# Cross-attention and ternary FFN on one core: work taken batch by batch, six product tiles transposed by DMA as int16

## What is computed (the reference, cut)

```
q = ctx @ Wq.T + bq; k = ctx @ Wk.T + bk
x = x + layernorm(x) @ softmax(q @ k.T).T            # both per batch
bit_linear(x, w, b):
    gx = max|x| per row; xq = round(x * 127 / gx) * gx / 127
    gw = mean|w|;        wq = clip(round(w / gw), -1, 1) * gw
    return xq @ wq.T + b
h = layernorm(x)
p = silu(bit_linear(h, gate_w, gate_b)) * bit_linear(h, val_w, val_b)
out = x + bit_linear(p, out_w, out_b)
```

## Time and profile before

| quantity | value |
|---|---|
| median of 3 runs | 69.74 us (69.73 to 70.26) |
| profiled execution: its time, its span | 69.72 us, 67.6 us |
| instructions | 1258 |
| busy: PE, DVE, ACT, POOL | 83%, 71%, 70%, 75% of the span |
| read from HBM, written to HBM | 6.04 MB, 1.05 MB |

### The profile page before, as it was taken

The page is one execution under the profiler, slowest core; times in us unless marked ns, Lnnn a source line. Parts: engine busy times, 40 slices in busy tenths (PEclk is TensorE's granted clock), DMA queues, the critical chain, the costliest instruction groups (busy, mean ns, idle before and its releaser), DMA issues.

```text
span 67.6 us, 1258 instructions
## 1 busy us (share of the span) xinstructions
PE 56.4 (83%) x353; PEld 36.2 (54%) x356; DVE 47.7 (71%) x140; ACT 47.4 (70%) x84; POOL 51.0 (75%) x108
## 2 busy tenths in 40 slices
PE   3999959798977896359799999999999999999500
PEld 2775649486847683232335433453844547988300
DVE  2002338896599957199898899999999988965500
ACT  5311479999996998398878867579689596995000
POOL 5904990688849877897997869868999999999100
PEclk9999999999999999999999999999999999999999
DMA  0899999999951000000000000000000000006354
GB/s 0 194 336 248 361 255 315 393 422 422 410 196 43 10 5 0 5 0 0 0 5 0 0 0 0 0 0 0 0 10 0 0 0 0 0 0 200 112 172 146
DMA packets 3254, 7.20 MB, mean 107 GB/s; under 512 B 392, under 2 KB 1836, under 8 KB 3248
## 3 DMA queue, kind: packets, MB, share of 16 engines
q1 hardware_dynamic: 3248, 7.13, 30.5%
HBM read 6.04 MB, written 1.05 MB: 105 GB/s over the span
## 4 chain that ended last, share of the span: by engine, by line
PE 48%; DMA 16%; POOL 12%; SPq 8%; DVE 5%; issue 4%; DVEq 0%; POOLq 0%
DMA x<-in_x_tok 16%; PE psG L750 11%; PE psV L750 10%; PE psO L827 7%; PE psT L798 5%; SPq L196 4%; PE psH L827 4%; PE psV L745 3%; PE psG L745 3%; POOL prob L279 3%; POOL rstd L289 2%; DVE st L385 2%; PE psV L785 2%; POOL rstd L269 2%; PE psH L734 1%
## 5 line engine op out<-in xcount | busy, mean ns | idle before, releaser
L608 ACT ACTIVATE sil<-psG,s_gv 128x1024 f32<-128x1024 f32 x8 | 8.9, 1113 | 1.8 <-PE psG L750 1.6
L494 DVE TENSOR_REDUCE pmax<-prod 128x1 f32<-128x1024 f32 x8 | 9.5, 1208 | 0.0
L481 DVE TENSOR_TENSOR prod<-psV,sil 128x1024 f32<-128x1024 f32 x7 | 8.6, 1222 | 0.8 <-PE psV L750 0.7
L617 ACT ACTIVATE pT<-psT,unshift 128x1024 bf16<-128x1024 f16 x7 | 7.8, 1113 | 1.8 <-PE psT L798 1.3
L750 PE MATMUL psG<-ter_gate,hT 128*128 128x512 bf16 x29 | 7.6, 381 | 0.5 <-issue 0.3
L329 POOL TENSOR_SCALAR prod<-prod,pqs 128x1024 f32<-128x1024 f32 x7 | 7.8, 1115 | 0.0
L750 PE MATMUL psV<-ter_val,hT 128*128 128x512 bf16 x28 | 7.3, 382 | 0.0
L279 POOL TENSOR_SCALAR prob<-prob,resum 128x256 f32<-128x256 f32 x8 | 3.7, 475 | 3.4 <-DVE resum L397 3.4
L324 POOL TENSOR_TENSOR res<-x,bo_sb 128x256 f32<-128x256 f32 x8 | 5.7, 740 | 0.0
L680 PE MATMUL psT<-kT,qT 128*128 128x256 f32 x16 | 4.2, 392 | 1.3 <-ACT qT L557 1.3
L827 PE MATMUL psO<-ter_out,pT 128*128 128x256 bf16 x40 | 5.2, 273 | 0.0
(11 more groups left out here) (121 smaller groups left out, 148.0 us busy)
## 6 DMA issues: line engine op xcount, KB each, us to landing
w_gate<-in_w_gate SPq DMA_DIRECT2D x2, 512.0 KB, 5.9
x<-in_x_tok SPq DMA_DIRECT2D x2, 512.0 KB, 10.0
xt_sb<-in_x_T SPq DMA_DIRECT2D x2, 512.0 KB, 10.7
w_val<-in_w_val SPq DMA_DIRECT2D x2, 512.0 KB, 11.0
w_out<-in_w_out SPq DMA_DIRECT2D x2, 512.0 KB, 12.7
out_x<-res SPq DMA_DIRECT2D x8, 128.0 KB, 1.8
ctx_sb<-in_ctx_T SPq DMA_DIRECT2D x1, 384.0 KB, 3.9
bias_rows<-bh_part SPq DMA_DIRECT2D x9, 4.0 KB
```

The costliest lines, as they stand in the source:

```text
L481: nc.vector.tensor_tensor(prod[:, t % P_RING, :], psV[:], sil[:, t % S_RING, :], ALU.mult).then_inc(prod_done, 1)
L494: nc.vector.tensor_reduce(pmax[:, t:t + 1], prod[:, t % P_RING, :], AX.X, ALU.max, apply_absolute_value=True).then_inc(pmax_done, 1)
L608: nc.scalar.activation(sil[:, t % S_RING, :], psG[:], ACT.Silu, scale=s_gv[:, t, 0:1]).then_inc(sil_done, 1)
L617: nc.scalar.activation(pT[:, t % T_RING, :], psT_h[t % 2], ACT.Identity, bias=unshift[:]).then_inc(pT_sb, 1)
```

## The change

- Loads: SP asks for ctx of batch 0, of 1, of 2 and 3, then x of each of the first two batches, xt of batch 0, w_gate, the output bias, x of the other two batches; then comes `spread_bias`, which waits for POOL, and behind it xt of batches 1 and 2, w_val, half of w_out, xt of batch 3 and the other half. wqk and bh are asked for by ACT's queue.
- Attention goes batch by batch. `k_out` moves from DVE to ACT, `normalise` of batches 0 and 1 from POOL to DVE. `centre_x` is gone: the shift is added at the end (`scale_product`'s bias for tiles 0 to 4, `add_bias_shift` on POOL for tiles 5 to 7). Two memsets move from POOL to DVE.
- FFN: the scale steps of h are recast, `inverse_parts(0)` moves to DVE. The products with the hidden biases follow those of gate and precede those of value (`biases`).
- Tiles 0 to 5 (NDMA = 6): POOL writes the rounded product as int16 to one of 4 buffers (`p_round_int`), SP issues one transposing DMA of 128x1024 int16 from SBUF to SBUF (`turn`), and the result is widened to bf16 on DVE (tiles 0, 2, 4) or ACT (1, 3, 5). Tiles 6 and 7 go through PE as before.
- EARLY becomes 5; products 0 to 4 use one PSUM bank, psO.
- All five lists are reordered. The diff, cut to its core:

```diff
+    S_RING, P_RING, T_RING, I_RING = 3, 5, 3, 4
+    EARLY = 5
+    NDMA = 6
@@ sync
+            def turn(t):
+                sp.wait_ge(pround_done[t], 1)
+                if t >= I_RING:
+                    sp.wait_ge(pT_sb[t - I_RING], 1)
+                sp.dma_start_transpose(pT_int[:, t % I_RING], p_int[:, t % I_RING, :]).then_inc(turned[t], 16)
...
+            load_ctx(0, 0, 1); load_ctx(1, 1, 2); load_ctx(2, 2, 4); load_x(0, 0, 2); load_x(1, 2, 4);
+            load_xt(0, 0, 1); load_w(0, 0); load_w(0, 1); load_bo(); load_x(2, 4, 6); load_x(3, 6, 8);
+            spread_bias(); load_xt(1, 1, 2); load_xt(2, 2, 3); load_w(1, 0); load_w(1, 1); load_w(2, 0);
+            load_xt(3, 3, 4); load_w(2, 1); turn(0); turn(1); turn(2); turn(3); turn(4); turn(5); store(0);
+            store(1); store(2); store(3); store(4); store(5); store(6); store(7)
@@ gpsimd
+            def p_round_int(t):
+                pool.wait_ge(pqs_done, t + 1)
+                if t >= I_RING:
+                    pool.wait_ge(turned[t - I_RING], 16)
+                nc.gpsimd.tensor_scalar(p_int[:, t % I_RING, :], prod[:, t % P_RING, :], pqs[:, t:t + 1], 1.0,
+                                        ALU.mult, ALU.mult).then_inc(pround_done[t], 1)
...
+            inverse_parts(2); p_round_int(0); inverse_parts(3); scale_out(0); h_round(6); h_round(7);
+            p_round_int(1); add_bias(4); scale_out(1); to_int(2, 1); add_bias_shift(5); p_round_int(2);
+            p_round_int(3); scale_out(2); scale_out(3); p_round_int(4); p_round_int(5); add_residual(0);
+            add_bias_shift(6); scale_out(4); scale_out(5); p_round(6); add_bias_shift(7); add_residual(1);
+            add_residual(2); add_residual(3); add_residual(4); scale_out(6); scale_out(7)
@@ vector
+            def widen(t):
+                dve.wait_ge(turned[t], 16)
+                if t >= T_RING:
+                    dve.wait_ge(o_done, t - T_RING + 1)
+                nc.vector.tensor_copy(pT[:, t % T_RING, :],
+                                      pT_int[:, t % I_RING].rearrange("p k m -> p (k m)")).then_inc(pT_sb[t], 1)
...
+            row_max(0); stats_x(0, 2); row_max(1); invert_sum(0); normalise(0); stats_x(2, 4); row_max(2);
+            invert_sum(1); normalise(1); row_max(3); invert_sum(2); add_x(0); stats_x2(0); add_x(1); mean_x2(0);
...
+            stats_x2(6); stats_x2(7); mean_x2(6); scales_h(1); mean_x2(7); clip(1, 0); clip(1, 1); h_max(2);
+            h_max(3); scale_h(2); times_value(0); scale_h(3); p_max(0); scales_h(2); gamma_p(0); times_value(1);
+            invert_gamma_p(0); scales_h(3); p_max(1); times_value(2); gamma_p(1); gamma_w(2); p_max(2);
+            invert_gamma_p(1); scales_w(2); gamma_p(2); times_value(3); invert_gamma_p(2); p_max(3); widen(0);
+            times_value(4); clip(2, 0); clip(2, 1); p_max(4); gamma_p(3); gamma_p(4); invert_gamma_p(3);
+            times_value(5); invert_gamma_p(4); p_max(5); gamma_p(5); invert_gamma_p(5); times_value(6);
+            widen(2); p_max(6); gamma_p(6); widen(4); invert_gamma_p(6); times_value_half(0);
+            times_value_half(1); p_max(7); gamma_p(7); invert_gamma_p(7); p_round_half(1); add_residual(5);
+            p_copy_half(1); add_residual(6); add_residual(7)
@@ scalar
+            centre_x2(6); centre_x2(7); silu(0); abs_sum(2, 0); silu(1); h_copy(2); abs_sum(2, 1); h_copy(3);
+            silu(2); h_copy(4); silu(3); to_int(2, 0); h_copy(5); silu(4); h_copy(6); h_copy(7); silu(5);
+            widen(1); scale_product(0); silu(6); scale_product(1); widen(3); silu(7); scale_product(2);
+            widen(5); scale_product(3); p_copy(6); p_round_half(0); scale_product(4); p_copy_half(0)
@@ tensor
+            att_transpose(3); apply_att(3); h_transpose(0); h_transpose(1); gate(0); biases(0); value(0);
+            gate(1); biases(1); h_transpose(2); value(1); h_transpose(3); gate(2); biases(2); value(2);
+            weight_sum(2); h_transpose(4); gate(3); biases(3); value(3); h_transpose(5); gate(4); biases(4);
+            value(4); h_transpose(6); gate(5); h_transpose(7); biases(5); value(5); last_product(0); gate(6);
+            biases(6); value(6); last_product(1); gate(7); biases(7); last_product(2); value(7);
+            last_product(3); p_transpose(6); last_product(4); last_product(5); p_transpose_half(0);
+            p_transpose_half(1); last_product(6); last_product(7)
```

More of the change, by code:

```diff
@@ L160, in xattn_ffn @@
[L160 to L164, removed]
+        q_ps, k_ps = sem("q_ps"), sem("k_ps")
+        q_sb, k_sb = sem("q_sb"), sem("k_sb")
@@ L169, in xattn_ffn @@
[L169 removed]
+        abs_done, wsum_done, gw_done, rgw_done = (sem(n) for n in ("abs_done", "wsum_done", "gw_done", "rgw_done"))
+        int_done = [[sem(f"int_done_{w}{z}") for z in range(2)] for w in ("gate", "val", "out")]
+        ter_done = sem("ter_done")
         gate_done, val_done, sil_done, prod_done, pmax_done = (sem(n) for n in (
             "gate_done", "val_done", "sil_done", "prod_done", "pmax_done"))
[L173 to L174 removed]
@@ L178, in xattn_ffn @@
+        turned = [sem(f"turned{t}") for t in range(NDMA)]
         val_half, round_half, pT_ps_half, pT_sb_half = ([sem(f"{n}{i}") for i in range(2)] for n in (
@@ L203, in _ @@
[L203 to L223, removed]
-                sp.dma_start(out_t[:, t, :], res[:, t, :]).then_inc(stored, 16)
+            def load_ctx(i, a, e):
+                sp.dma_start(ctx_sb[:, a * S:e * S], ctx_T[:, a * S:e * S]).then_inc(l_ctx[i], 16)
@@ L535, in _ @@
-            scale_h(0); h_max(1)
-            add_x(4); clip(1, 0); gamma_h(1); invert_gamma_h(1); scales_h(1); clip(1, 1)
-            add_x(5); add_x(6); scale_h(1); stats_x2(4); stats_x2(5); stats_x2(6); mean_x2(4); mean_x2(5)
-            times_value(0); h_max(2); gamma_h(2); mean_x2(6); invert_gamma_h(2); add_x(7); scales_h(2)
-            times_value(1); stats_x2(7); scale_h(2); p_max(0); mean_x2(7); times_value(2); gamma_w(2)
-            gamma_p(0); scales_w(2); invert_gamma_p(0); p_max(1); times_value(3); h_max(3); gamma_h(3)
@@ L558, in q_out, with k_out @@
                                      bias=wqk_sb[:, 2 * DH:2 * DH + 1]).then_inc(q_sb, 1)
+            def k_out(b):
+                act.wait_ge(k_ps, b + 1)
+                nc.scalar.activation(kT[:, b * S:(b + 1) * S], ps_k[b], ACT.Identity,
+                                     bias=wqk_sb[:, 2 * DH + 1:2 * DH + 2]).then_inc(k_sb, 1)
             def exps(b):
@@ L617, in p_copy, with widen @@
                 nc.scalar.activation(pT[:, t % T_RING, :], psT_h[t % 2], ACT.Identity,
-                                     bias=unshift[:]).then_inc(pT_sb, 1)
+                                     bias=unshift[:]).then_inc(pT_sb[t], 1)
+            def widen(t):
+                act.wait_ge(turned[t], 16)
+                if t >= T_RING:
+                    act.wait_ge(o_done, t - T_RING + 1)
+                nc.scalar.copy(pT[:, t % T_RING, :],
+                               pT_int[:, t % I_RING].rearrange("p k m -> p (k m)")).then_inc(pT_sb[t], 1)
             def scale_product(t):
@@ new lines, in value @@
+            def value(t):
+                if t < LAST:
+                    for k in range(KD):
+                        if t == 0:
+                            pe.wait_ge(ter_done, 3 + k)
+                        for c in range(2):
+                            mm = nc.tensor.matmul(psV[:, c * HC:(c + 1) * HC], hT[:, t, k, :],
+                                                  w_ter[1][:, k * HID + c * HC:k * HID + (c + 1) * HC],
+                                                  start=False, stop=(k == KD - 1))
+                    mm.then_inc(val_done, 1)
```

466 lines of the change are left out of this document (237 added, 229 removed).

## The result

The change took the kernel from 69.85 us (69.73 to 70.26, 4 runs) to 66.97 us (65.99 to 68.83, 4 runs), so the ratio of the medians is 0.959. The forecast was 65.8 us, the range 64.0 to 74.0. The profiled execution took 67.32 us with a span of 65.5 us.

What follows compares the result with a forecast made beforehand. Bound by DMA up to 17.7 us, then a chain between engines, then TensorE and VectorE both full from 30.1. PE 58.3, DVE 59.0, POOL 58.8; ties 1.0, residual 0.6, tail 2.9: span 63.7, time 65.8 us, range 64.0 to 74.

Steps and rivals of the forecast that it cites:

- The front: Everything up to DVE's first product: times_value(0) near 31.6 us against 32.34, a gain of 0.7 us.
- The danger: SP's list: xt of batches 1 to 3 and w_val behind nine issues waiting for POOL; cover 1 to 4 us.
- The second rival: Bias DMAs hold w_val and xt 3 us beyond cover; times_value(0) 3 us later, 68.8 us; chance 0.14.
- DVE's stretch: FFN, from times_value(0) to the last inverse on DVE: 23.9 us, 2.7 less than before.
- From the last inverse to the last residual's end: End of FFN: ACT's rounding and copy, transposes, last product, handovers, ties; last product ends at 60.2, residual takes 0.6.
- The tie: End of FFN: PE, DVE and POOL meet within 0.7 us, for which 1.0 us was added.
- The tail and what lies outside: Last residual's end to span's end: 2.9 us, between 2.3 and 3.6; beyond the span, 2.12 us as in the profiled execution.
- The turn: FFN tiles 0 to 5, transposing DMA: 3.0 us to landing, 1.5 to 3 us between turns.
- The first rival's sum: Slow turns one after another on one queue end the FFN slower; span equals the old at R = 3.4; chance 0.20.
- R: Microseconds per turn in the slow-turns span; 4.5 gives 73.9 us and 6.5 gives 85.9 us.
- the 10.5 us for a turn: FFN turns: estimate from the skill's 1309 ns per block, were a turn's eight blocks to go one after another.

Runs made afterwards that it cites:

- the three groups: Follow-up runs on separate occasions, each beside the unchanged kernel before, whose median there was 69.97, 69.34 and 70.31 us.
- the first experiment: Kernel after, with SP asking for xt of batches 1 and 2 and w_val before the nine bias DMAs: 64.86 us, ratio 0.950.
- The doubled turns: Kernel with the bias transfers moved, each turn preceded by a spare turn of the same tile into an unread buffer: 70.64 us.
- three edits together: Kernel with bias transfers moved, plus silu(7) before widen(3), POOL rounding tile 2 earlier, and scale_out(6) and (7) earlier on POOL: 65.51 us.
- the third round early: Kernel after, with POOL rounding tile 2 ahead of add_bias(4) and add_bias_shift(5): 68.37 us, ratio 0.987.
- on the steady front: The same early rounding of tile 2, on the kernel with the bias transfers moved behind w_val: 64.76 us, ratio 0.938.
- the attention first: Kernel after, with att_transpose(3) and apply_att(3) ahead of weight_sum(1) in TensorE's list: 70.89 us.

## Why the prediction was right, and where its terms were off

The sign and the mechanism held: six transposes less on PE, turns that are mostly hidden, a DVE with more work in the first 17.7 us. Against the profiled execution's 67.32 us the forecast of 65.8 is 1.5 us short, and the terms differ by more than that, with both signs: 1.8 and 2.1 us too little, 1.3 and 1.1 too much. That they cancel to 1.5 is luck.

- **The front: 1.8 us short.** times_value(0) was priced at 31.6 and came at 33.39. It is 3.0 us short from the first row maximum on (priced 31.6 - 8.39 = 23.2, measured 26.24); 1.2 us of the miss is hidden by luck, since this execution had its first row maximum at 7.15. The step "Its value is held by DVE's own queue and not by a load" is the one that failed. The danger and its place were named (SP's nine issues ahead of w_val), but not its size: I had w_val landing near 19 and wanted at 20.3. xt of batch 1 was asked for at 13.78 and w_val at 14.73, much as forecast (near 14 for xt); what was mis-sized is the landing, some 4 us without a row for it, where w_val's two transfers took 7.3 us (median) and ACT got its halves at 21.65 and 22.93. That is also the condition I gave under which I would be wrong (the second weight after 21 us). The second rival is thus the one that came true, in part. The experiment with the bias transfers moved shows it: 30.96, and 64.86 us. What I had not priced at all is the clock: it falls after PE's idle time for the weight, and the last apply_att takes 3.38 us and not 1.97. That the idle time brings it down is read from the order of events: in the five traces with the lower level in the front PE had just been idle for 1.5 to 3.0 us, and in the six with the loads moved there is neither such a pause nor the lower level in the front. No run forced the pause alone, and a pause of that size isn't enough by itself: in the second trace of the kernel before PE idles for 1.80 us before 8.80 and the clock stays at 1.00. Nor does the clock account for the whole spread of the runs. The kernel before, without this wait, spreads over 2.9 to 4.4 us in the three groups, two runs of the kernel after with the same mean clock (0.974) took 66.62 and 67.32 us, and in the first experiment two of the four runs have a mean clock of 0.97 at no loss.
- **DVE's stretch: 2.1 us short.** Priced 23.9, measured 25.99. Busy time is 24.34, so 0.4 is mis-sized work: the two clips took 1.38 in place of 0.8. The other 1.65 us is idle time, of which 1.34 lies in four waits, 0.79 for turns and 0.55 for silus. With silu(7) ahead of widen(3) the stretch fell by 0.8: the sentence "ACT is less patient: widen(3) stands before silu(7)" had the right place and too much cover (3 us; it waited 1.37, where no wait over 1 us was forecast).
- **From the last inverse to the last residual's end: 1.3 us too much.** Priced 5.3 (59.0 - 55.5, plus 1.0 for ties, 0.2 to be on 60.2, and 0.6), measured 63.38 - 59.38 = 4.0. The tie was priced at 1.0 us and cost 0.2 at most. The engines did meet as closely as forecast:
```profile
60.91 0.69 ACT L699 ACTIVATE pT<-psT,unshift 128x512 bf16<-128x512 f16 x1
...
61.82 1.04 PE L892 MATMUL psH<-ter_out,pT 128*128 128x256 bf16 x8
...
61.61 0.65 POOL L376 TENSOR_SCALAR s_o<-pgam,s_gv,gw 128x1 f32<-128x1 f32 x2
```
  ACT's last copy ends at 61.60, and PE starts the last product at 61.82, straight after the one before it. POOL's last scale_outs end at 62.26, ahead of the last residual at 62.90. PE's idle 2 us lie earlier, between 45 and 60 as forecast.
- **The tail and what lies outside: 1.1 us too much.** 65.5 - 63.38 = 2.1 against 2.9, since no issue of a store stalled (570 ns at most), and 1.82 against 2.12 outside of the span.
- **The turn.** Priced 3.0 us to landing, between 1.8 and 6.5. Alone it takes 3.0, in a bunch up to 4.5. The first rival's sum (45 + 4R + 8.8) takes turns to run one after another; their issues do, at 1.3 us, but one turn's movement goes on beside the next one's issue, so the last four (issued at 48.90, 50.18, 51.85 and 53.66) are 1.3 to 1.8 us apart and not 3 to 4.5, close to the pace of POOL's rounds. R in that sum is nearer 1.6, and that is the pace at which the turns were asked for. The doubled turns show what a larger R does: 70.64 us.

The Trainium skill's "DMA: Bandwidth & Descriptors" (Latency and other measured facts) gives 261 GB/s as the effective rate of a transposing DMA with a non-contiguous middle dimension; 0.26 MB in about 1.3 us is 200 GB/s here, somewhat below. "VectorE: DVE Perf Modes" (The three transpose paths) gives 1309 ns a block by DMA; eight blocks in one DMA land in 3.0 us, so this case contradicts it read as a serial price, and the 10.5 us for a turn did not come.

**What to carry to other kernels.** Before a list is changed, write down for each load when its issue can start, with the small transfers ahead of it at their full issue time (here 0.56 us each, nine of them 5 us); a load's start is as much a step of the path as its movement. A transfer that stands in for engine work pays when no wait for it stands ahead of work that another engine needs: moving one silu ahead of one wait took 0.8 us off DVE's stretch. Where PE falls idle ahead of long matmuls, price them at the lower clock as well: eight of them took 3.38 us here in place of 1.97. And count from the first work that every version shares, not from the start of the span.

## What was not expected of the hardware

- A transposing DMA within SBUF of 128x1024 int16 costs SP's queue 1.23 to 1.72 us to issue (median 1.30), moves in about 1.3 us as some 1024 pieces over all 16 engines, and lands 3.0 to 4.5 us after its issue starts.
- A DVE pass from int16 to bf16 over 128x1024 takes 0.43 us, and 1.24 us with POOL's passes over 1024 columns running beside it (three edits together, above), though it has no wait before it. With the third round early it took 0.94 and, on the steady front, 1.20, with the attention first 1.33. POOL is busy beside the short ones too, so that POOL is the cause, or which of its passes, stays open.
- A store's issue took 2.01 us in one execution of the kernel before (62.34 to 64.35, with the DMA share at 0.2 from 63 on) and 1.15 in another, and at most 0.57 after. What holds it stays open.
